# One block for the input projection and the scan of a Mamba layer, the scan's first tiles loaded during the dt stage, the norm's chain in another order

## The reference, cut to what matters

```
x, z = split(hidden @ in_proj_w)                      # input projection
xc = silu(conv4(x) + conv_b)                          # per channel, 4 taps
dt_r, Bm, Cm = rmsnorm of three slices of xc @ x_proj_w.T
dt = softplus(dt_r @ dt_proj_w.T + dt_bias)           # "dt stage"
h[t] = exp(dt[t] * A) * h[t-1] + dt[t] * Bm[t] * xc[t]   # the scan
ys[t] = sum over the states of h[t] * Cm[t]
out = ((ys + D * xc) * silu(z)) @ out_proj_w.T
```

## Time and profile before

| what | us |
|---|---|
| median of 3 runs (lowest, highest) | 3373.0 (3372.03, 3375.18) |
| the profiled execution | 3373.22 |
| its span, first to last instruction | 3371.9 |
| granted TensorE clock, mean | 0.942 |
| PE busy, share of the span | 3003.7, 89% |
| DVE busy | 2148.4, 64% |
| ACT busy | 1471.8, 44% |
| POOL busy | 1431.5, 42% |

### The profile page before, as it was taken

How to read it: one execution, slowest core, us unless ns; L and a number is a source line. 1 busy time by engine, 2 the same in 40 slices (tenths; PEclk the granted TensorE clock), 3 DMA queues, 4 the chain that set the end, 5 groups by cost and what they waited for, 6 DMA issues and landing times. The chain is left out here.

```text
span 3371.9 us, 36262 instructions
## 1 busy us (share of the span) xinstructions
PE 3003.7 (89%) x12619; PEld 2169.8 (64%) x12619; DVE 2148.4 (64%) x1659; ACT 1471.8 (44%) x2392; POOL 1431.5 (42%) x826
## 2 busy tenths in 40 slices
PE   9995477877877799997999999978899999999996
PEld 7861133333333487886888888867688888888884
DVE  6558899999999556325777777755633433334336
ACT  4446455555555443213888888833312112112111
POOL 0004899999999332303888888810100000000001
PEclk9995689999999899998999999989899999999998
DMA  3225975656565473322111111153111111111101
GB/s 142 86 70 208 259 172 133 163 144 147 134 167 139 142 256 117 113 87 68 36 36 34 34 34 37 35 190 101 61 35 59 45 43 56 50 37 62 50 6 63
DMA packets 158962, 324.60 MB, mean 96 GB/s; under 512 B 28173, under 2 KB 40205, under 8 KB 157741
## 3 DMA queue, kind: packets, MB, share of 16 engines
q1 hardware_dynamic: 142126, 314.86, 31.0%
q10 hardware_dynamic: 16704, 8.09, 0.9%
HBM read 250.21 MB, written 72.68 MB: 96 GB/s over the span
## 5 line engine op out<-in xcount | busy, mean ns | idle before, releaser
L752 POOL TENSOR_TENSOR scan_dbx<-scan_u,scan_b_bc 128x1024 f32<-128x1024 f32 x256 | 595.5, 2365 | 22.7 <-DMA scan_u<-u 22.7
L1606 POOL TENSOR_TENSOR at_p_lo<-at_p,at_p_hi 128x512 fp32r<-128x512 f32 x384 | 516.4, 1351 | 143.0 <-ACT at_p_hi L1510 131.8
L955 POOL TENSOR_TENSOR ff_y<-ff_y,ff_rstd 128x512 f32<-128x512 f32 x14 | 24.9, 1807 | 1125.5 <-DVE ff_rstd L944 1125.5
L700 ACT ACTIVATE scan_ps_a<-scan_dt,scan_a_neg 128x512 f32<-128x512 f32 (+1 forms) x512 | 331.8, 680 | 274.4 <-DVE scan_g L715 254.4
L726 DVE TENSOR_TENSOR_SCAN scan_ps_a<-scan_ps_a,scan_dbx 128x1024 f32<-128x1024 f32 x192 | 432.3, 2281 | 0.3 <-ACT scan_ps_a L702 0.3
L1551 DVE TENSOR_REDUCE at_neg_max<-at_ps 128x1 fp32r<-128x1536 f32 x132 | 231.8, 1757 | 142.8 <-PE at_ps L1627 140.7
L827 PE MATMUL scan_ps_y<-scan_g,scan_sel 128*32 128x512 f32 x1024 | 151.8, 665 | 174.0 <-DVE scan_g L715 166.1
L2027 DVE TENSOR_TENSOR ff_hf<-ff_sg,ff_ps_u 128x1024 f32<-128x1024 f32 x28 | 34.2, 1221 | 388.5 <-PE ff_ps_u L98 388.5
L1507 ACT ACTIVATE at_p<-at_ps 128x512 f32<-128x512 f32 x384 | 227.9, 594 | 104.6 <-PE at_ps L1644 84.2
L1510 ACT ACTIVATE at_p_hi<-at_p 128x512 fp32r<-128x512 f32 x384 | 242.8, 632 | 12.3
L715 DVE TENSOR_TENSOR scan_g<-scan_ps_a,scan_c_bc 128x1024 f32<-128x1024 f32 x192 | 230.4, 1201 | 0.0
(11 more groups left out here) (244 smaller groups left out, 7196.3 us busy)
## 6 DMA issues: line engine op xcount, KB each, us to landing
scan_dt<-dt SPq DMA_DIRECT2D x128, 256.0 KB, 4.7
scan_u<-u SPq DMA_DIRECT2D x128, 256.0 KB, 7.7
ff_w<-in_w SPq DMA_DIRECT2D x56, 512.0 KB, 4.3
mid_first_w<-in_w_out SPq DMA_DIRECT2D x32, 512.0 KB, 5.1
ff_w<-in_w SPq DMA_DIRECT2D x56, 256.0 KB, 2.6
ff_wo_wo<-in_w_o SPq DMA_DIRECT2D x32, 384.0 KB, 3.1
in_w<-in_w_in SPq DMA_DIRECT2D x18, 512.0 KB, 3.2
xc<-xc SPq DMA_DIRECT2D x16, 512.0 KB, 2.8
```

Of the source, the lines that this page charges most:

```text
L700: nc.scalar.activation(at[:, h * L + h:(h + 1) * L], dt[it % 2][:, c, h:L], ACT.Exp, scale=a_neg[:, it % IT, e:e + 1]).then_inc(a_ready, 1)
L752: nc.gpsimd.tensor_tensor(dbx[n % SL][:].rearrange("p (h l) -> p h l", h=2), u[it % 2][:, c:c + 2], b_bc[:, b, k // 2].unsqueeze(1).to_bro ...
L1606: nc.gpsimd.tensor_tensor(p_lo[t % NSL][:], p[t % NSL][:], f32(p_hi[t % NSL][:]), ALU.subtract).then_inc(p_lo_done, 1)
```

## The change

`mamba_in` and `mamba_scan` become functions that return streams. A new function `mamba` writes one block in which each engine runs its stream of the projection and then that of the scan. There is no block end and no clearing of semaphores between them; the 54 semaphores of the projection are cleared by SP in the scan, at `it == 4`. All of PSUM is one tensor of 8 banks that both share. The scan's buffers lie at addresses that are free by the time that they are written, and waits on `r_done` and `dt_done` guard the PSUM banks. SP loads the rows of B and C, dt(0), xs(0), u(0), dt(1) and u(1) of the scan between stores of the dt stage. POOL computes the first three `dbx` before its last u(15). In the norm's chain the last `xproj` moves into `main(16)` ahead of its last k, ACT's copy `gate(16)` goes behind `ssm` and `sq`, and `mean_squares` moves in `main(17)` from k = 4 to k = 1. ACT's groups are tile 0 alone, the pairs (1,2) to (13,14), and tile 15 alone.

The diff, without the re-indentation (whitespace at the line's start is not compared):

```diff
-            for i in range(0, IT, 2):
+        for group in ([0], *([i, i + 1] for i in range(1, IT - 1, 2)), [IT - 1]):
+            for i in group:
                 exponentials(i)
-                exponentials(i + 1)
+            for i in group:
                 logarithm(i)
-                logarithm(i + 1)
...
             next_w(IT, 0)
-            gate(IT, 0)
             act.wait_ge(xproj_done, XP_LAST)
...
             nc.scalar.activation(sq, ps_xp, ACT.Square).then_inc(sq_done, 1)
+        gate(IT, 0)
             act.wait_ge(ms_done, 1)
...
-            main(IT, 0)
-            xproj(1, IT, stop=True)
+        main(IT, 0, lambda: xproj(1, IT, stop=True), HT - 1)
...
-            main(IT + 1, 1, mean_squares)
+        main(IT + 1, 1, mean_squares, 1)
...
                 sp.dma_start(u[i], uu[i % 2][:]).then_inc(u_st[i % 2], 16)
+            if i == 1:
             sp.wait_ge(xc_st, 16 * IT)
             sp.wait_ge(bc_st, 16)
+                scan.load_rows(sp, 0)
+            for it in range(2):
+                if i == it + 2:
+                    sp.wait_ge(dt_st[it], 16)
+                    scan.load_dt(sp, it)
+                    if it == 0:
+                        scan.load_xs(sp, it)
             for s in range(2):
                 sp.wait_ge(z_st[s], 16 * (NT - IT) // 2)
+                    sp.wait_ge(u_st[it], 16)
+                    scan.load_u(sp, it)
...
             for i in range(IT):
+            if i == IT - 1:
+                pool.wait_ge(bc_st, 16)
+                for n in range(scan.early):
+                    scan.product(pool, n)
                 pool.wait_ge(dt_done, i + 1)
...
+        sp.wait_ge(before.dt_done, IT)
+        load_xs(sp, 1)
             sp.dma_start(wk[:], d["w_k"]).then_inc(wk_ld, 16)
...
                     free_a(n - SA)
+            else:
+                act.wait_ge(before.r_done, IT - 2 + n)
...
+def mamba(nc, res, d):
...
+    ps_all = res.bank("mamba_ps", [P, 8, L])[:]
+    scan = mamba_scan(nc, res, d, ps_all)
+    early = Phase(nc)
+    first = mamba_in(nc, early, d, ps_all, scan)
...
+    with nc.Block() as block:
+        @block.sync
+        def _(sp):
+            first.sync(sp)
+            scan.sync(sp, first, early.release)
...
-    phase(mamba_in, d)
-    phase(mamba_scan, d)
+    phase(mamba, d)
```

More of the change, by code:

```diff
@@ L13 @@
+from collections import namedtuple
 from contextlib import ExitStack
@@ L495, in mamba_scan, with at @@
-    ps_y = res.bank("scan_ps_y", [P, L])
-    ps_x = res.bank("scan_ps_x", [P, L])
+    def at(k):
+        return Arena(nc, "scan", BASE + 1024 * k)
+    late = TOP - 4 * B * IT * L
+    wk, wv, cx = at(0)("wk", [P, HT, KW]), at(12)("wv", [P, HT, KW]), at(24)("cx", [P, HT, TOKS])
+    b_bc, c_bc = ([at(k + 8 * row)(f"{n}{b}", [P, NB, L]) for b, k in enumerate((121, 32))] for row, n in enumerate(("b_bc", "c_bc")))
+    wz = [at(48 + 4 * s)(f"wz{s}", [P, HT, P]) for s in range(ZC)]
+    dt = [at((72, 56)[s])(f"dt{s}", [P, CG, L]) for s in range(2)]
@@ new lines, in mamba_scan @@
+    u = [at((80, 88)[s])(f"u{s}", [P, CG, L]) for s in range(2)]
+    small = at(64)
+    kb = [small(f"kb{s}", [P, TOKS]) for s in range(2)]
+    vb = [small(f"vb{s}", [P, KW]) for s in range(2)]
+    dbx_at = Arena(nc, "scan", at(96).at + 64)
+    dbx = [dbx_at(f"dbx{s}", [P, 2 * L]) for s in range(SL)]
+    par = Arena(nc, "scan", late - 6 * 1024)
+    a_neg, a_exp = par("a_neg", [P, IT, NS]), par("a_exp", [P, IT, NS])
+    d_p, ident, sel = par("d_p", [P, IT]), par("ident", [P, P]), par("sel", [P, CW])
@@ new lines, in mamba_scan @@
+    d_diag = [par(f"d_diag{s}", [P, P]) for s in range(2)]
+    xs = [par("xs0", [P, L]), small("xs1", [P, L])]
+    assert par.at <= late and small.at <= at(72).at
+    last = Arena(nc, "scan", late)
+    g = [last(f"g{s}", [P, 2 * L]) for s in range(SG)]
+    x = last("x", [P, HT, TOK])
+    yb = [last(f"yb{s}", [P, L]) for s in range(2)]
+    zb = [last(f"zb{s}", [P, L]) for s in range(2)]
+    ps_a = [ps_all[:, m:m + 2].rearrange("p n l -> p (n l)") for m in (6, 0, 4)]
+    ps_y, ps_x = ps_all[:, 2], ps_all[:, 3]
@@ L519, in mamba_scan @@
     BEHIND = SL - 1
+    EARLY = 3
     def by_pool(n):
@@ new lines, in gpsimd, with times_c @@
+    def gpsimd(pool):
+        def times_c(n):
+            v = g[n % SG][:].rearrange("p (h l) -> p h l", h=2)
+            b = n // (NP // B)
+            pool.wait_ge(c_ld[b], 16 * CG)
+            pool.wait_ge(scanned, n + 1)
+            nc.gpsimd.tensor_tensor(v, v, c_bc[b][:, n % NK // 2].unsqueeze(1).to_broadcast([P, 2, L]),
+                                    ALU.mult).then_inc(g_pool, 1)
+        for n in range(NP):
+            if n >= EARLY:
+                product(pool, n)
+            if n >= BEHIND and by_pool(n - BEHIND):
+                times_c(n - BEHIND)
@@ L703, in _ @@
[L703 to L706 removed]
+            first.scalar(act)
+            scan.scalar(act, first)
         @block.vector
         def _(dve):
[L710 to L718 removed]
@@ L743, in _ @@
[L743 to L756 removed]
+            first.gpsimd(pool)
@@ L841 @@
+            first.tensor(pe)
+            scan.tensor(pe, first)
 class Norm:
```

952 lines of the change are left out of this document (460 added, 492 removed).

## The result

The changed kernel takes 3351.3 us (median of 4 runs, 3347.0 to 3355.6) where the kernel before takes 3372.5 beside it (4 runs, 3370.0 to 3375.2). The ratio is 0.9937, 95% interval 0.9920 to 0.9954: 21 us (0.6%) faster, by the interval 16 to 27. The forecast was 3354, with 3343 to 3361.

What follows compares the result with a forecast made beforehand. DVE was taken to set the time from the first softplus tile to the scan's end. Terms -27.4 + 2.4 - 4.3 + 10.2 = -19.1 us, from 3373.2 to 3354 us; range 3343 to 3361, about 8 in 10.

Steps and rivals of the forecast that it cites:

- The hole: DVE's 27.51 us without work between the dt stage and the scan closes to about 0.1 us: -27.4 us.
- The head: First scan steps: u(15) between POOL's products puts step 4 at +13.9 us instead of 11.53 after step 0: +2.4 us.
- The norm's chain: Ahead of the dt stage: earlier mean_squares, no PE pause, r(1) (DVE, dt tile 1) at 247.0 instead of 251.32: -4.3 us.
- that rival: Table switches on ACT cost 2.66 us each, as on the skill's page; ln(1)'s chain 5.5 us longer, 3360 us; chance 0.01.
- The stores behind the loads: dt stage: stores queue behind moved loads in SP's queue, r(7) 3.1 us late and r(8) 7.2: +10.2 us together.
- The walk: Step-by-step timing of SP's in-order queue after u(1)'s store, through loads and stores: dt(3) lands at 283.5, dt(4) at 295.6.
- The queue hides the loads: Rival: reads and writes in one queue overlap, stall 4.2 us or none, 3348 or 3344 us; chance 0.30.
- The forecast's turns: SP's queue serves transfers one after another: 1.27 us per 512 KB store, 1.19 us per 256 KB load.
- The slow mix: Rival: loads beside stores run at 186 GB/s, stall 15.6 us, 3359 us, up to 3366; chance 0.11.
- little gain: Rival: loads at 150 GB/s, stall 23.7 us, gain 5.6 us, within what a measurement can tell; chance 0.05.
- a loss: Rival: loads under about 132 GB/s, stall 29.3 us or more, slower than before; 3383 us at 110 GB/s; chance 0.04.
- DVE free of waits in the scan's body: Sign expected in the trace after the change: DVE does not wait in the body of the scan; no size given.

Runs made afterwards that it cites:

- Run 8: Changed kernel with POOL's first three scan products set apart, one behind each of u(12), u(13), u(14): 3351.4 us, ratio 0.9940.
- Run 12: Changed kernel with the norm's chain back in its old order, ACT's groups and the loads as changed: 3357.4 us, ratio 0.9956.
- run 1: Kernel before plus only the new norm's chain and ACT's new groups, blocks and loads as before: 3368.7 us, ratio 0.9992.
- run 10: Changed kernel with ACT's old groups, pairs (0,1), (2,3) and so on: 3351.8 us, ratio 0.9943.
- Run 3: Changed kernel with the 8 loads of dt(1) and u(1) moved behind the dt stage, 17 of 25 staying early: 3346.0 us, ratio 0.9927.
- run 4: Changed kernel with the same 25 loads spread, one behind each store from tile 1 on: 3342.4 us, ratio 0.9915.
- run 7: Changed kernel with the 25 loads issued in ACT's DMA queue, SP's queue keeping the stores alone: 3346.4 us, ratio 0.9922.
- run 5: Changed kernel with the 25 loads spread, two behind each store from tile 1 on: 3341.2 us, ratio 0.9908.
- run 2: Changed kernel with all 25 loads behind the dt stage's last store and POOL's first products behind u(15): 3361.1 us, ratio 0.9973.
- run 11: Changed kernel with one load behind each store, POOL's three products set apart and ACT's old pairs: 3339.3 us, ratio 0.9906.
- run 6: Changed kernel with the 25 loads spread, four behind each store from tile 1 on: 3350.1 us, ratio 0.9930.
- run 9: Changed kernel with one load behind each store and POOL's three first products set apart: 3339.1 us, ratio 0.9903.

## Why the prediction was right, step by step

- **The hole, -27.4.** Right: no idle time at 329.60 against 27.51.
- **The head, +2.4.** Right: step 4 starts 13.83 us after step 0 (forecast 13.9; its terms add up to 13.8), 11.53 before, so +2.3, in two waits for POOL. Run 8 removes it.
- **The norm's chain, -4.3.** Right: -4.46 for r(1). PE and ACT show the steps:

```profile
220.60 1.88 PE L430 MATMUL mamba_ps<-in_acc,in_meanw 96*96 96x512 f32 x4
...
231.87 5.31 PE L440 MATMUL mamba_ps<-in_pre,in_dtw_dtw 65*128 65x512 f32 x12
...
233.79 1.02 ACT L292 ACTIVATE in_tail_ee<-mamba_ps 128x1024 f32<-128x1024 f32 x1 [0.69 <-PE mamba_ps L440]
234.83 1.28 ACT L294 ACT_TABLE_LOAD   x1
236.13 1.06 ACT L294 ACTIVATE in_tail_ee<-in_tail_ee 128x1024 f32<-128x1024 f32 x1
```

`mean_squares` stands at 220.60, 220.2 on the old clock (the copy is 0.37 later). PE begins the first dt product without a pause, and ACT reads it 1.92 us later, the 1.9 of the upper level; the granted clock is 0.94 in 231 to 242 and 0.50 after. Run 12 gives 4.71 for the chain alone, run 1 gives 4.46 for chain and groups; the new groups themselves are no gain for r(1), which comes 0.79 sooner with the old pairs (run 10). The table load at 234.83 is followed by exp at 236.13, 1.30 us again and not the 2.66 of the Trainium skill, ScalarE: Activation LUTs, "What ACT_TABLE_LOAD costs": that rival is out.
- **The stores behind the loads, +10.2.** Right in place and size: 4.15 in r(7) and 6.63 in r(8), 10.8 in all, forecast 3.1 and 7.2. The walk holds in its steps too: counted from r(1), dt(3) landed after 33.3 us and dt(4) after 44.8, forecast 32.2 and 44.3. Run 3 ties the second wait to the last eight loads, runs 4 and 7 the whole to bunches in the one queue. The walk left out that SP itself is held up at its issues; in a queue that is served in turns this changed no landing.
- **Sum, -19.1.** At the last scan instruction -18.66. The medians differ by 21.2; the 2.5 more are within the spread of 8.6 us between runs. The profiled execution, at 3347.0, gained 26.2, of which 7.9 lie behind the last scan instruction, in code that is the same. In the 14 profiled executions that stretch lasts 2239.5 to 2248.1 us, and the changed kernel's is the shortest of all; no run ties these us to the change.
- **The rivals.** "The queue hides the loads" (0.30, 3344 to 3348) did not come about with bunches of 8 and 9, but run 5 shows that it was not empty: pairs of loads between stores cost DVE nothing. The forecast's turns held since its loads stood in bunches. The prediction had no row on the mix and said so, so part of the close hit is luck: with other orders of the same loads its walk is 0.8 to 2.9 us off. The slow mix, little gain and a loss are out: the loads ran at about the 220 GB/s assumed.

What the prediction did not have is ACT in the scan. It said "DVE free of waits in the scan's body", and there is one of 1.71 us, in DVE's timeline and behind these rows of ACT's:

```profile
375.00 2.30 DVE L750 TENSOR_TENSOR_SCAN mamba_ps<-mamba_ps,scan_dbx 128x1024 f32<-128x1024 f32 x1 [1.71 <-ACT mamba_ps L727]
```

```profile
372.12 0.38 ACT L664 ACTIVATE scan_kb<-mamba_ps 128x256 f32<-128x256 f32 x1 [2.91 <-PE mamba_ps L797]
373.22 0.40 ACT L656 ACTIVATE scan_d_diag<-scan_ident,scan_d_p 128x128 f32<-128x128 f32 x1 [0.72 <-PE mamba_ps L841]
373.53 1.28 ACT L725 ACTIVATE mamba_ps<-scan_dt,scan_a_neg 128x512 f32<-128x512 f32 x2
```

ACT takes its work in order; its copy of a key tile waited 2.91 us for PE, and the factors of a scan step stood behind it. Here it cost little, since the kernel before loses nearly as much to a wait for ACT, later in the scan:

```profile
994.43 2.29 DVE L726 TENSOR_TENSOR_SCAN scan_g<-scan_ps_a,scan_dbx 128x1024 f32<-128x1024 f32 x1 [1.32 <-ACT scan_ps_a L702]
```

## What to carry to other kernels

Loads that are moved into a stage with stores are paid for by what stands behind them in the queue: spread them, one or two behind each store, and count for each buffer that is written again how long its store may take (here stores that landed up to 12.7 us after their issue cost nothing; one that was issued 12 us late and landed after 14.8 stopped VectorE for 6.6). Closing a hole between two stages is worth the hole less the waits that its loads bring; write both into the sum, queue by queue. A gain of 1 to 3 us at the head of a long pipelined stage has to be read again at the stage's end, since another engine's in-order queue may take it back.

## What the runs showed of the hardware

- A DMA share near 1 does not say what moves. The same loads and stores in one queue moved 264 GB/s with loads in bunches of 8 and 9 (turns would give 264), 275 in fours (266) and 317 in pairs (291), and about 400 with loads and stores in two queues (281). The Trainium skill, DMA: Bandwidth & Descriptors, "Issuing engines are not separate DMA queues", says that a second issuing engine saves only the time of the issue, since all share the same 16 DMA engines. By that run 7 should have moved its bytes no faster than one queue does. It moved 398 GB/s of a mix for which turns at the two rates measured alone give 281, so for loads beside stores the measurement differs.
- The Trainium skill, DMA: Bandwidth & Descriptors, "Two DMAs through the same engine are not ordered", has separate read and write sides in an engine. The partial overlap of neighbours in one queue fits it; no run here shows the mechanism.
- The issue itself slows down when the queue is deep: four loads took SP 1.92 us at 258.74 and 5.27 at 267.47. From there to 277.25 13 or 14 transfers of the changed kernel were issued and not landed at every issue, and the issues came no faster than the landings. On an engine that also computes that is a stall, 5.93 us on ACT in run 7.
- Waits of 1.0 to 1.9 us for ACT come and go in the scan between kernels that differ only ahead of it (none longer than 0.6 us in runs 2, 4, 5 and 11, one in the kernel before, the changed kernel and runs 3, 10 and 12, two in runs 6 to 9, three in run 1). That a copy of ACT stands behind PE there is in the trace of the changed kernel; what decides in which kernel it happens stays open.
